# Self-attention inside a fused transformer block: heads that leave the matmul already turned

## The chip, the cores and the metric

The kernel runs on one core of a Trainium2 chip, as one launch. The metric is the device time in microseconds (us), the median of several executions.

## The reference

A block of 1024 tokens (32 sequences of 32 tokens, width 1024) in float32 passes through cross-attention, self-attention and a gated feed-forward part, each with a layer norm ahead of it and a residual sum behind it. The change is in the self-attention:

```python
q = (x @ Wq.T).reshape(B, S, H, dk).transpose(0, 2, 1, 3)     # 16 heads of 64
k = (x @ Wk.T).reshape(B, S, H, dk).transpose(0, 2, 1, 3)
v = (x @ Wv.T).reshape(B, S, H, dk).transpose(0, 2, 1, 3)
scores = jnp.einsum('bhqd,bhkd->bhqk', q, k) / jnp.sqrt(jnp.float32(dk))
scores = jnp.where(causal, scores, jnp.finfo(scores.dtype).min)
probs = jax.nn.softmax(scores, axis=-1)
attn = jnp.einsum('bhqk,bhkd->bhqd', probs, v)
attn = attn.transpose(0, 2, 1, 3).reshape(B, S, D)
return attn @ Wo.T
```

## The kernel before

**Tiling.** The tokens are 8 tiles (NT) of 128: four sequences of 32 tokens each. The 16 heads are 4 groups (NG) of four heads (HG). The loop over groups is a loop of the program for the first three; the last group is written out, because the layer norm of the feed-forward part (statistics, normalising, turning) is woven into it (`last`). Large matmuls take each operand as two parts of type fp32r, a high and a low one, and multiply them in three matmuls (`three`). The small ones of the attention (scores, attend, transposes) are in float32, and the trace records two passes for each float32 matmul, one for each transpose.

**A group on TensorE.** Queries and keys for all tokens (`job`, 24 matmuls of 512 columns each), then a pipeline over the tiles. In step st:

- `turn_heads(st - 2)`: two transposes of `o_sb`, into the second half of bank 4
- `scores(st)`: four heads, two passes each, stationary `qT`, moving `kT`, 64 rows of the array by turns
- `values(st + 1)`: v of the next tile, in bank 5
- `attend(st - 1)`: four heads, stationary the turned probabilities `att_z` (128 columns), moving `v` (64 columns), into the first half of bank 4
- `project(st - 2)`: 12 matmuls of 512 columns, `oT_hi` and `oT_lo` against the output weights, into banks 6 and 7

Step 7 has no `values`, and there `project(5)` stands ahead of `attend(6)`. After it come the first job of the next group, cut in two by `turn_heads(6)`, then `attend(7)`, `project(6)`, `turn_heads(7)`, the second job and `project(7)`. In the last group each step from 3 on ends with `norm_tile(st - 3)`, which turns a normalised tile.

**VectorE in step st** (all engines work through their queue in order, and wait on semaphores): `oT_lo` of tile st - 2, adding the causal mask to the scores (line 1446, four instructions), the row maximum (line 1451), a wait for ACT's exponentials, the turning of the probabilities (line 1461, four instructions), the reciprocal of the sums (line 1463), the division of the heads of tile st - 1 into `o_sb` (line 1473), and the addition of the projection of tile st - 2 to x (line 1481, two instructions), which frees banks 6 and 7 (`wo_free`). In the last group the statistics, part of the normalising and `xT_lo` come on top.

**ACT in step st:** `oT_hi` of tile st - 2 (line 687), the exponentials with their sums (line 669, four heads), the copy of v out of bank 5 (line 676), in some steps the high part of a weight tile.

A single `oT_hi` and `oT_lo` serve all tiles. The split of weights into low parts is GpSimd's.

Of the kernel before, what the change touches and what calls it, by code (L numbers as in the profile page):

```python
# [48 lines left out]
def build(nc, x_in, ctx_in, w_in, block_in, mask_in, ext_in, ext_t_in, out):  # L49
    stack = ExitStack()  # L50
    with stack:
# [74 lines left out]
        o_sb = sb(s, "o_sb", [P, HG * DK])  # L126
        oT_hi = sb(s, "oT_hi", [P, FT, P], F32R)
        oT_lo = sb(s, "oT_lo", [P, FT, P], F32R)
# [87 lines left out]
        o_ready = sem("o_ready")  # L216
        oT_psum = sem("oT_psum")
# [65 lines left out]
        TURNED_HEADS = slice(HG * DK, HG * DK + FT * P)  # L283
# [274 lines left out]
        def _(act):  # L558
# [104 lines left out]
            def group(g, last=False):  # L663
                def exps(st):

                    act.wait_ge(att_top_ready, g * 8 + (st + 1))
                    rowsof = flat3(att[st % 2])
                    for h in range(HG):
                        ins = act.activation(att_p[st % 2][:, h, :], rowsof[:, h * S:(h + 1) * S], ACT.Exp,  # L669
                                             bias=att_neg[st % 2][:, h:h + 1],  # L670
                                             accum_out=att_sum[st % 2][:, h:h + 1])
                    ins.then_inc(att_exp, 1)

                def keep_values(t):
                    act.wait_ge(v_done, g * 8 + (t + 1))
                    act.activation(v[:, t, :], ps[:, 5, 0:HG * DK], ACT.Copy).then_inc(v_kept, 1)

                keep_queries(g, 2)
                keep_queries(g, 3)
                pair_split(g, 2)  # L680
                act.wait_ge(k_done, g * 4 + 4)
                pair_split(g, 3)
                keep_values(0)
                for st in range(NT + 2):
                    if st >= 2:
                        act.wait_ge(oT_psum, g * 8 + (st - 1))
                        act.activation(flat(oT_hi[:, :, :]), ps[:, 4, TURNED_HEADS], ACT.Copy)\
                            .then_inc(oT_hi_done, 1)
                    if last and st >= 4:
                        turned_hi(2, st - 4)  # L690
                    if st < NT:
                        exps(st)
                    if st + 1 < NT:
                        keep_values(st + 1)
                    if last and st % 2 == 0 and st >= 4:
                        normalise(2, st - 3)
                    if st + 1 == NT - 1:
                        pair_split(g, 4)
                if not last:
                    keep_queries(g + 1, 0)  # L700
                    act.wait_ge(wo_done, (g + 1) * NT)
                    pair_split(g, 5)
                    keep_queries(g + 1, 1)
# [138 lines left out]
        def _(pe):  # L842
# [169 lines left out]
            def group(g, last=False):  # L1012
# [21 lines left out]
                def turn_heads(t):  # L1034

                    pe.wait_ge(o_ready, g * 8 + (t + 1))
                    for f in range(FT):
                        mm = pe.transpose(ps[:, 4, (FT + f) * P:(FT + f + 1) * P],
                                          o_sb[:, f * P:(f + 1) * P], ident[:, :])
                    mm.then_inc(oT_psum, 1)  # L1040

                def attend(t):
# [6 lines left out]
                    for h in range(HG):  # L1049
                        mm = pe.matmul(ps[:, 4, h * DK:(h + 1) * DK],  # L1050
                                       att_z[t % 2][:, (h % 2) * 2 + h // 2, :],
                                       v[:, t, h * DK:(h + 1) * DK], start=True, stop=True)
                    mm.then_inc(pv_done, 1)

                def project(t):
# [5 lines left out]
                    for f in range(FT):  # L1061
                        for half in range(2):
                            at = f * D + half * HALF
                            mm = three(ps[:, 6 + half, :], (oT_hi[:, f, :], oT_lo[:, f, :]),
# [15 lines left out]
                for st in range(2, NT):  # L1080
                    if st > 2:
                        turn_heads(st - 2)
                    pe.wait_ge(att_read, g * 8 + st)
                    scores(g, st)
                    if st == 2:
                        turn_heads(0)
                    if st < NT - 1:
                        values(st + 1)
                        attend(st - 1)
                        project(st - 2)  # L1090
                    else:
                        project(st - 2)
                        attend(st - 1)
# [7 lines left out]
                turn_heads(NT - 2)  # L1101
                mm = job(0, 0, 0, range(4, KD))
                if not last:
                    mm.then_inc(q_done, 1)
                attend(NT - 1)
                project(NT - 2)
                if last:
                    norm_tile(2, NT - 3)
                turn_heads(NT - 1)
                if last:  # L1110
                    job(1, 0, 1, range(0, 3))
                else:
                    job(1, 0, 1).then_inc(q_done, 1)
                project(NT - 1)
                if last:
                    norm_tile(2, NT - 2)

# [126 lines left out]
        def _(dve):  # L1244
# [182 lines left out]
            dve.memset(att_inv[0][:, :], 0.0).then_inc(wo_free, 1)  # L1427
            def group(g, last=False):
# [4 lines left out]
                for st in range(NT + 2):  # L1433
                    two = st % 2
                    if st >= 2:
                        dve.wait_ge(oT_hi_done, g * 8 + (st - 1))
                        dve.tensor_tensor(flat(oT_lo[:, :, :]), ps[:, 4, TURNED_HEADS],
                                          flat(oT_hi[:, :, :]).bitcast(F32), ALU.subtract)\
                            .then_inc(oT_ready, 1)
# [14 lines left out]
                    if last and st >= 4:  # L1454
                        turned_lo(2, st - 4)
                    if st < NT:
                        dve.wait_ge(att_exp, g * 8 + (st + 1))
                        for b in range(BT):
# [4 lines left out]
                        mark(dve.reciprocal(att_inv[two][:, :], att_sum[two][:, :]))  # L1463
                        settle()
# [4 lines left out]
                    if 1 <= st <= NT:  # L1469
                        dve.wait_ge(pv_done, g * 8 + st)  # L1470

                        by = att_inv[(st - 1) % 2][:, :].rearrange("p (e h) -> p h e", e=2)
                        dve.tensor_tensor(o_sb[:, :].rearrange("p (h e d) -> p h e d", h=2, e=2),
                                          ps[:, 4, 0:HG * DK].rearrange("p (h e d) -> p h e d", h=2, e=2),
                                          by.unsqueeze(3).broadcast_to([P, 2, 2, DK]), ALU.mult)\
                            .then_inc(o_ready, 1)
                    if st >= 2:
                        dve.wait_ge(wo_done, g * 8 + (st - 1))
                        for half in range(2):
                            part = x[:, st - 2, half * HALF:(half + 1) * HALF]  # L1480
                            ins = dve.tensor_tensor(part, ps[:, 6 + half, :], part, ALU.add)
                        ins.then_inc(wo_free, 1)
                        if last and st == NT + 1:
# [4 lines left out]
                        if last:  # L1488
                            dve.wait_ge(wo_free, g * 8 + st)
                            tile_stats(st - 2)  # L1490
# [153 lines left out]
GROUP_MARKS = 8  # L1644
# [82 lines left out]
```

## Time and profile before

| what | value |
|---|---|
| time, median of 3 runs | 1565.85 us (1565.71 to 1567.55) |
| profiled execution, time | 1564.08 us |
| its span, first to last instruction | 1562.3 us |
| TensorE busy | 97% of the span |
| VectorE, ACT, GpSimd busy | 51%, 34%, 54% |
| mean granted clock of TensorE | 0.997 |

The span is what the trace covers; the time is what the device reports for that same execution. Busy shares are means over the whole program. In the trace the matmuls of one line are pipelined, so each record lasts longer than the distance from its start to the next one's: costs on TensorE are read from start to start.

### The profile page before, as it was taken

To read this page: it belongs to the slowest core of one execution; us is meant where nothing else is said; L and a number is where in the kernel's file an instruction comes from. 1 tells how busy PE (TensorE), PEld (TensorE's weight loads), DVE (VectorE), ACT (ScalarE), POOL (GpSimd) and SP (SyncE) were. 2 spreads that over 40 slices of the span, in tenths; PEclk is the share of its full clock that TensorE was granted. 3 is DMA by queue.
4 is the path that set the end of the run, shared out by engine and by line. 5 is a ranking of instruction groups with operands and counts; after the bars stand their busy time and mean duration, and the time that the engine had idled before them with its cause. 6 is when DMAs were issued, how large, how long until landed. Compare 5 with 4: busy or idle time off the path is not lost.

```text
span 1562.3 us, 23574 instructions
## 1 busy us (share of the span) xinstructions
PE 1519.8 (97%) x8204; PEld 1246.1 (80%) x8204; DVE 795.9 (51%) x1249; ACT 536.7 (34%) x1093; POOL 851.4 (54%) x658
## 2 busy tenths in 40 slices
PE   6999899999999999989999999999999999999998
PEld 5667688888888887878888888888888888888886
DVE  4666516236145168694365365266266256256346
ACT  3334412222122133334334333433343443343342
POOL 0000220221211212167987987887887897897895
PEclk9999999999999999999999999999999999999999
DMA  9663210110100100011211211211211211111122
GB/s 367 261 243 149 108 54 29 54 54 19 61 27 27 54 1 1 21 34 54 74 47 42 72 47 54 60 47 54 60 51 49 60 54 47 60 54 49 58 60 107
DMA packets 41798, 110.42 MB, mean 71 GB/s; under 512 B 4672, under 2 KB 4800, under 8 KB 39328
## 3 DMA queue, kind: packets, MB, share of 16 engines
q1 hardware_dynamic: 41328, 109.07, 20.7%
q10 hardware_dynamic: 432, 0.82, 0.2%
q8 instruction: 27, 0.44, 0.1%
q14 instruction: 11, 0.09, 0.0%
HBM read 105.68 MB, written 4.19 MB: 70 GB/s over the span
## 4 chain that ended last, share of the span: by engine, by line
PE 89%; DVE 7%; ACT 1%; issue 1%; DMA 1%; SPq 0%; POOL 0%; DVEq 0%
PE ps L1212 36%; PE ps L1232 18%; PE ps L844 8%; PE ps L846 7%; PE ps L845 7%; PE ps L875 3%; PE ps L922 2%; PE ps L898 2%; PE ps L1050 1%; PE ps L850 1%; DVE t_raw L1533 1%; DMA x<-in_x 1%; ACT att_p L669 1%; DVE att L1446 1%; DVE att_z L1461 1%
## 5 line engine op out<-in xcount | busy, mean ns | idle before, releaser
L485 POOL TENSOR_TENSOR b_lo<-blk,b_hi 128x512 fp32r<-128x512 f32 x180 | 238.9, 1334 | 53.3 <-ACT b_hi L739 44.7
L454 POOL TENSOR_TENSOR w_lo<-raw,w_hi 128x2048 fp32r<-128x2048 f32 x18 | 83.5, 4640 | 325.7 <-ACT w_hi L604 325.7
L1616 DVE TENSOR_TENSOR x<-ps,x 128x1024 f32<-128x1024 f32 x210 | 242.2, 1210 | 0.0
L1212 PE MATMUL ps<-xT_hi,b_hi 128*128 128x512 f32 x480 | 187.0, 389 | 2.1 <-DVE x L1519 2.1
L1212 PE MATMUL ps<-xT_lo,b_hi 128*128 128x512 f32 x480 | 186.8, 389 | 0.0
L1212 PE MATMUL ps<-xT_hi,b_lo 128*128 128x512 f32 x480 | 186.7, 389 | 0.0
L1232 PE MATMUL ps<-b_hi,b_hi 128*128 128x512 f32 x420 | 166.7, 397 | 0.1
L1232 PE MATMUL ps<-b_lo,b_hi 128*128 128x512 f32 x420 | 163.7, 390 | 0.0
L1232 PE MATMUL ps<-b_hi,b_lo 128*128 128x512 f32 x420 | 163.6, 389 | 0.0
L1590 DVE TENSOR_TENSOR hid<-ps,kept 128x512 f32<-128x512 f32 x60 | 41.5, 691 | 229.6 <-PE ps L1212 189.7
L485 POOL TENSOR_TENSOR b_lo<-s_sum,b_hi 128x512 fp32r<-128x512 f32 x105 | 137.8, 1313 | 32.0 <-ACT b_hi L739 32.0
L1593 DVE TENSOR_TENSOR ps<-ps,kept 128x512 f32<-128x512 f32 x60 | 41.7, 694 | 181.7 <-PE ps L1212 152.8
L844 PE MATMUL ps<-xT_hi,w_hi 128*128 128x512 f32 x320 | 126.1, 394 | 0.0
L846 PE MATMUL ps<-xT_hi,w_lo 128*128 128x512 f32 x320 | 124.6, 390 | 0.0
L845 PE MATMUL ps<-xT_lo,w_hi 128*128 128x512 f32 x320 | 124.6, 389 | 0.0
L739 ACT ACTIVATE b_hi<-s_sum 128x512 fp32r<-128x512 f32 x105 | 66.1, 630 | 170.0 <-POOL s_sum L494 161.3
L739 ACT ACTIVATE b_hi<-blk 128x512 fp32r<-128x512 f32 x180 | 110.5, 622 | 22.6 <-PE ps L1212 19.7
L1212 PEld LDWEIGHTS ps<-xT_hi,b_hi 128*128 128x128 f32 x480 | 90.1, 188 | 21.6 <-DVE x L1519 2.9
L1212 PEld LDWEIGHTS ps<-xT_hi,b_lo 128*128 128x128 f32 x480 | 90.1, 188 | 18.7
L1212 PEld LDWEIGHTS ps<-xT_lo,b_hi 128*128 128x128 f32 x480 | 90.1, 188 | 18.7
L1232 PEld LDWEIGHTS ps<-b_hi,b_hi 128*128 128x128 f32 x420 | 78.8, 188 | 26.0 <-DVE x L1616 5.5
L762 ACT ACTIVATE kept<-ps 128x512 f32<-128x512 f32 x90 | 53.6, 596 | 131.9 <-PE ps L1212 131.9
(167 smaller groups left out, 3302.8 us busy)
## 6 DMA issues: line engine op xcount, KB each, us to landing
blk<-in_blocks SPq DMA_DIRECT2D x180, 256.0 KB, 2.7
ctx<-in_ctx SPq DMA_DIRECT2D x64, 512.0 KB, 9.4
raw<-in_w SPq DMA_DIRECT2D x19, 1024.0 KB, 4.8
x<-in_x SPq DMA_DIRECT2D x8, 512.0 KB, 4.1
out<-x SPq DMA_DIRECT2D x16, 256.0 KB, 2.6
xn<-in_ext ACTq DMA_DIRECT2D x3, 128.0 KB, 8.0
mask<-in_mask ACTq DMA_DIRECT2D x1, 288.0 KB, 6.7
extT<-in_ext_t ACTq DMA_DIRECT2D x1, 128.0 KB, 4.6
```

Of the source, the lines that this page charges most:

```text
L454: pool.tensor_tensor(w_lo[wslot][:, :], raw[slot][:, :], w_hi[wslot][:, :].bitcast(F32), ALU.subtract).then_inc(split_done[slot], 1)
L485: pool.tensor_tensor(b_lo[slot][:, :], src[:, :], b_hi[slot][:, :].bitcast(F32), ALU.subtract).then_inc(block_lo, 1)
L739: act.activation(b_hi[w_slot(n)][:, :], src[:, :], ACT.Copy).then_inc(block_hi, 1)
L762: act.activation(kept[i][:, :], ps[:, Y, :], ACT.Copy).then_inc(part_kept, 1)
L844: pe.matmul(dst, stat[0], moving[0], start=start, stop=False)
L845: pe.matmul(dst, stat[0], moving[1], start=False, stop=False)
L846: return pe.matmul(dst, stat[1], moving[0], start=False, stop=stop)
L875: mm = pe.transpose(ps[:, b, e * MB + m * P:e * MB + (m + 1) * P], ctx[t % RING][:, b, j // 2, m, at:at + P], ident[:, :])
L1212: mm = pe.matmul(ps[:, bank, :], stat[a], moving[b], start=first and m == 0, stop=(s == 3 and m == 2), skip_group_check=True)
L1232: mm = pe.matmul(ps[:, DOWN_BANKS[place] + i, :], stat[a], moving[b], start=DOWN_STARTS[place] and m == 0, stop=m == 2, skip_group_check=True)
L1593: dve.tensor_tensor(ps[:, Y + to, :], ps[:, Y + bank, :], kept[k][:, :], ALU.add)\
L1616: dve.tensor_tensor(part, ps[:, bank:bank + 2, :], part, ALU.add).then_inc(down_added, 1)
```

## The change

In `attend` the operands swap places: `v` of a head (64 columns) is stationary and the turned probabilities (128 columns) move, so that the result comes out as features by tokens, two heads above each other in the 128 partitions. `turn_heads`, `o_sb` and their semaphores go. VectorE divides the probabilities by their sum before it turns them, where it divided the heads afterwards. `oT_hi` and `oT_lo` get two buffers each. ACT copies `oT_hi` right behind `attend`, one step earlier in its order, and VectorE's `oT_lo` follows in the same step. In the first three groups the addition to x moves from the end of step st (tile st - 2) to the middle of the next (tile st - 3, behind the maximum); in the last group it stays. On TensorE `attend` stands ahead of `project` in all steps, the first job of the next group is cut differently, and `project(7)` comes ahead of the second job in the first three groups.

```diff
-        TURNED_HEADS = slice(HG * DK, HG * DK + FT * P)
+        HEADS = slice(0, FT * P)
...
                 for st in range(NT + 2):
-                    if st >= 2:
-                        act.wait_ge(oT_psum, g * 8 + (st - 1))
-                        act.activation(flat(oT_hi[:, :, :]), ps[:, 4, TURNED_HEADS], ACT.Copy)\
-                            .then_inc(oT_hi_done, 1)
...
                     if st + 1 < NT:
                         keep_values(st + 1)
+                    if 1 <= st <= NT:
+                        act.wait_ge(pv_done, g * 8 + st)
+                        act.activation(flat(oT_hi[(st - 1) % 2][:, :, :]), ps[:, 4, HEADS], ACT.Copy)\
+                            .then_inc(oT_hi_done, 1)
...
-                def turn_heads(t):
-
-                    pe.wait_ge(o_ready, g * 8 + (t + 1))
-                    for f in range(FT):
-                        mm = pe.transpose(ps[:, 4, (FT + f) * P:(FT + f + 1) * P],
-                                          o_sb[:, f * P:(f + 1) * P], ident[:, :])
-                    mm.then_inc(oT_psum, 1)
-
                 def attend(t):
...
                     for h in range(HG):
-                        mm = pe.matmul(ps[:, 4, h * DK:(h + 1) * DK],
-                                       att_z[t % 2][:, (h % 2) * 2 + h // 2, :],
-                                       v[:, t, h * DK:(h + 1) * DK], start=True, stop=True)
+                        r = slice((h % 2) * DK, (h % 2 + 1) * DK)
+                        mm = pe.matmul(ps[r, 4, (h // 2) * P:(h // 2 + 1) * P], v[:, t, h * DK:(h + 1) * DK],
+                                       att_z[t % 2][:, (h % 2) * 2 + h // 2, :], start=True, stop=True)
                     mm.then_inc(pv_done, 1)
...
                 for st in range(2, NT):
-                    if st > 2:
-                        turn_heads(st - 2)
                     pe.wait_ge(att_read, g * 8 + st)
                     scores(g, st)
-                    if st == 2:
-                        turn_heads(0)
                     if st < NT - 1:
                         values(st + 1)
-                        attend(st - 1)
-                        project(st - 2)
-                    else:
-                        project(st - 2)
-                        attend(st - 1)
+                    attend(st - 1)
+                    project(st - 2)
...
                 job(0, 0, 0, range(0, 4))
-                turn_heads(NT - 2)
-                mm = job(0, 0, 0, range(4, KD))
-                if not last:
-                    mm.then_inc(q_done, 1)
                 attend(NT - 1)
                 project(NT - 2)
+                mm = job(0, 0, 0, range(4, KD))
                 if last:
                     norm_tile(2, NT - 3)
-                turn_heads(NT - 1)
-                if last:
                     job(1, 0, 1, range(0, 3))
                 else:
-                    job(1, 0, 1).then_inc(q_done, 1)
+                    mm.then_inc(q_done, 1)
                 project(NT - 1)
                 if last:
                     norm_tile(2, NT - 2)
+                else:
+                    job(1, 0, 1).then_inc(q_done, 1)
...
+            def add_projected(g, t):
+                dve.wait_ge(wo_done, g * 8 + (t + 1))
+                for half in range(2):
+                    part = x[:, t, half * HALF:(half + 1) * HALF]
+                    ins = dve.tensor_tensor(part, ps[:, 6 + half, :], part, ALU.add)
+                ins.then_inc(wo_free, 1)
...
+                    if not last and st >= 3:
+                        add_projected(g, st - 3)
                     if st < NT:
                         dve.wait_ge(att_exp, g * 8 + (st + 1))
+                        mark(dve.reciprocal(att_inv[two][:, :], att_sum[two][:, :]))
+                        settle()
+                        mark(dve.tensor_tensor(att_p[two][:, :, :], att_p[two][:, :, :],
+                                               att_inv[two][:, :].unsqueeze(2).broadcast_to([P, HG, S]),
+                                               ALU.mult))
+                        settle()
                         for b in range(BT):
                             q = slice(b * S, (b + 1) * S)

                             ins = dve.transpose(att_z[two][q, :, b * S:(b + 1) * S], att_p[two][q, :, :])
                         ins.then_inc(att_turned, 1)
...
                     if 1 <= st <= NT:
...
+                        dve.wait_ge(oT_hi_done, g * 8 + st)
+                        dve.tensor_tensor(flat(oT_lo[(st - 1) % 2][:, :, :]), ps[:, 4, HEADS],
+                                          flat(oT_hi[(st - 1) % 2][:, :, :]).bitcast(F32), ALU.subtract)\
+                            .then_inc(oT_ready, 1)
+                    if last and st >= 2:
+                        add_projected(g, st - 2)
```

## Rows read from the trace of the kernel before

**Rows 1.** The page, busy time and share of the span

```profile
PE 1519.8 (97%) x8204; PEld 1246.1 (80%) x8204; DVE 795.9 (51%) x1249; ACT 536.7 (34%) x1093; POOL 851.4 (54%) x658
```

**Rows 2.** Busy time by stretch: start:end length, engines, granted clock, DMA

```profile
226.70:300.40 73.70, 71.70 (x481) 63.12 (x480) 37.89 (x111) 20.29 (x83) 9.17 (x2) 1.00 0.08 30
...
545.80:626.50 80.70, 75.21 (x523) 66.06 (x521) 60.07 (x150) 29.29 (x92) 15.63 (x23) 1.00 0.00 1
```

**Rows 3.** Timeline of TensorE, one step: start, length, instruction

```profile
250.54 1.00 PE L1050 MATMUL ps<-v,att_z 128*128 128x64 f32 x8
251.35 0.47 PE L844 MATMUL ps<-w_hi,oT_hi 128*128 128x512 f32 x1
...
254.21 0.38 PE L1038 MATMUL ps<-ident,o_sb 128*128 128x128 f32 x2
254.52 0.71 PE L1000 MATMUL ps<-kT,qT 64*128 64x128 f32 x8
255.16 0.39 PE L844 MATMUL ps<-w_hi,xT_hi 128*128 128x256 f32 x1
...
258.14 0.33 PE L1050 MATMUL ps<-v,att_z 128*128 128x64 f32 x2
```

**Rows 4.** Timeline of TensorE, step 2 of the first group

```profile
237.94 0.71 PE L1000 MATMUL ps<-kT,qT 64*128 64x128 f32 x8
239.81 0.44 PE L1038 MATMUL ps<-ident,o_sb 128*128 128x128 f32 x2 [1.15 <-DVE o_sb L1473]
240.00 0.36 PE L844 MATMUL ps<-w_hi,xT_hi 128*128 128x256 f32 x1
```

**Rows 5.** Groups by line, attention stage: total, mean ns, idle before

```profile
L1481 DVE TENSOR_TENSOR x<-ps,x 128x512 f32<-128x512 f32 x64 | 41.2, 684 | 50.8 <-PE ps L846 50.8
...
L1050 PEld LDWEIGHTS ps<-v,att_z 128*128 128x128 f32 x256 | 32.0, 192 | 0.6
L1000 PE MATMUL ps<-kT,qT 64*128 64x128 f32 x256 | 22.9, 297 | 0.0
...
L1473 DVE TENSOR_TENSOR o_sb<-ps,att_inv 128x256 f32<-128x256 f32 x32 | 13.6, 424 | 10.2 <-PE ps L1050 9.3
L1437 DVE TENSOR_TENSOR oT_lo<-ps,oT_hi 128x256 fp32r<-128x256 f32 x32 | 13.3, 416 | 9.5 <-ACT oT_hi L687 9.5
...
L687 ACT ACTIVATE oT_hi<-ps 128x256 fp32r<-128x256 f32 x32 | 12.3, 384 | 104.7 <-PE ps L1038 104.7
...
L1463 DVE RECIPROCAL att_inv<-att_sum 128x4 f32<-128x4 f32 x32 | 5.7, 178 | 1.0
```

**Rows 6.** Cross-attention's scores: loads by line, then TensorE's timeline

```profile
L898 PEld LDWEIGHTS ps<-cT,xt 128*32 128x32 f32 x512 | 14.9, 109 | 11.9 <-issue 3.6 <-ACT cT L572 1.0
...
118.60 1.93 PE L898 MATMUL ps<-cT,xt 128*32 128x256 f32 x32
120.46 0.33 PE L875 MATMUL ps<-ident,ctx 128*128 128x128 f32 x1
```

**Rows 7.** Timeline of step 7 of the first group, TensorE and VectorE

```profile
277.32 0.71 PE L1000 MATMUL ps<-kT,qT 64*128 64x128 f32 x8
...
278.74 1.18 DVE L1446 TENSOR_TENSOR att<-ps,causal 32x128 f32<-32x128 f32 x4
279.95 0.29 DVE L1451 TENSOR_REDUCE att_neg<-att 128x4 f32<-128x128 f32 x1
...
281.64 1.26 DVE L1461 STREAM_TRANSPOSE att_z<-att_p 32x128 f32<-32x128 f32 x4 [1.40 <-ACT att_p L669]
```

**Rows 8.** Waits, attention stage: total us, times, longest

```profile
PE ps L844 <- DVE oT_lo L1437: 4.6, 5, 1.7
```

**Rows 9.** Timeline of the last group, VectorE and TensorE

```profile
583.08 1.29 DVE L1481 TENSOR_TENSOR x<-ps,x 128x512 f32<-128x512 f32 x2 [0.30 <-PE ps L846]
...
600.35 1.29 DVE L1481 TENSOR_TENSOR x<-ps,x 128x512 f32<-128x512 f32 x2 [0.42 <-PE ps L846]
...
608.89 1.09 PE L850 MATMUL ps<-ident,xn 128*128 128x128 f32 x8 [1.24 <-DVE xn L1419]
```

More of the change, by code:

```diff
@@ L125, in build @@
         att_inv = [sb(s, f"att_inv{i}", [P, HG]) for i in range(2)]
-        o_sb = sb(s, "o_sb", [P, HG * DK])
-        oT_hi = sb(s, "oT_hi", [P, FT, P], F32R)
-        oT_lo = sb(s, "oT_lo", [P, FT, P], F32R)
+        oT_hi = [sb(s, f"oT_hi{i}", [P, FT, P], F32R) for i in range(2)]
+        oT_lo = [sb(s, f"oT_lo{i}", [P, FT, P], F32R) for i in range(2)]
         s.close()
@@ L215, in build @@
         pv_done = sem("pv_done")
-        o_ready = sem("o_ready")
-        oT_psum = sem("oT_psum")
         oT_hi_done = sem("oT_hi_done")
@@ L1063, in project @@
                             at = f * D + half * HALF
-                            mm = three(ps[:, 6 + half, :], (oT_hi[:, f, :], oT_lo[:, f, :]),
+                            mm = three(ps[:, 6 + half, :], (oT_hi[t % 2][:, f, :], oT_lo[t % 2][:, f, :]),
                                        (w_hi[1][:, at:at + HALF], w_lo[1][:, at:at + HALF]),
@@ L1432, in group @@
                         .then_inc(k_kept, 1)
-                for st in range(NT + 2):
+                for st in range(NT + (2 if last else 3)):
                     two = st % 2
[L1435 to L1439, printed above, removed]
                     if st < NT:
@@ L1462, in group @@
                         ins.then_inc(att_turned, 1)
-                        mark(dve.reciprocal(att_inv[two][:, :], att_sum[two][:, :]))
-                        settle()
                     if last and st % 2 and st >= 3:
@@ L1469, in group @@
                     if 1 <= st <= NT:
[L1470 to L1483, printed above, removed]
+                        dve.wait_ge(oT_hi_done, g * 8 + st)
[4 more added lines that the diff above has]
+                        add_projected(g, st - 2)
+                        if st == NT + 1:
                             dve.wait_ge(hi_done, ATT_PAIRS + 2)
@@ L1487, in group @@
                                               ALU.subtract).then_inc(split_done[1], 1)
-                        if last:
-                            dve.wait_ge(wo_free, g * 8 + st)
-                            tile_stats(st - 2)
+                        dve.wait_ge(wo_free, g * 8 + st)
+                        tile_stats(st - 2)
             dve.wait_ge(z_zero, 2)
@@ L1640, in _ @@
                         add(c, place, q)
-GROUP_MARKS = 8
+GROUP_MARKS = 16
 def flat(ap):
```

## Prediction

> **What bounds the kernel now.** I read the page first, then the busy times by stretch, then TensorE's instructions in order of time through one group of heads, and last the waits of the same stretch. The page puts TensorE at 97% busy over the whole span [rows 1], so a gain has to come out of its queue, or out of the 42 us in which it idles. By stretch, the attention part of each of the first three groups (from the first `values` to the last `project`) takes 73.7 us with 2.0 us idle, and that of the last group 80.7 us with 5.5 us idle; the granted clock is 1.00 [rows 2]. So the stage stands at full clock, the higher of its two levels, and is paced by TensorE.
>
> One inner step in order of time [rows 3] shows what that queue is made of, from start to start: attend 0.81 (250.54 to 251.35), project 2.86, turn_heads 0.31, scores 0.64, values 2.98 (255.16 to 258.14). Together 7.60 us, with no gap. Steps 3 to 6 of every group look like it, with a norm_tile more in the last group.
>
> **Removed: turn_heads.** 32 of them (8 tiles, 4 groups) at 0.31 us each: 9.9 us, 2.48 us a group. They stand bare on TensorE's path. With it goes the first one's wait: turn_heads(0) starts at 239.81, but scores(2) before it starts at 237.94 and needs 0.64, so TensorE was free at 238.58: 1.23 us a group [rows 4]. What takes its place is values(3), which needs bank 5 read by ACT, behind exps(1), behind VectorE. By the changed order VectorE finishes that chain about 0.3 us later than now (0.56 us added ahead of the first transposes, 0.21 taken from behind them), while TensorE arrives 0.17 us earlier: I take a new wait of 0.3 us. Net 0.9 us a group.
>
> **Changed: attend.** Now 4 heads, two passes each, so 8 records, with a 128-column stationary side and 64 moving columns. They run at 0.10 us a record, while a load of 128 columns lasts 0.192 and one of 32 columns 0.109 [rows 5, 6]: the loads seem to set the pace, not the columns that move. After: a stationary side of 64 columns, 128 moving, the heads alternating between the two column halves of the array. No row shows this form. The nearest is scores: also 8 records with 128 moving columns, alternating between two halves (of rows): 0.64 us [rows 3]. The readout's scores with 32-column stationary sides and 256 moving run 32 records in 1.86 us (118.60 to 120.46), 0.058 each [rows 6], twice the columns in half the time that attend's records take: column groups do overlap. I take 0.64, a saving of 0.17 an attend. Bounds: 8 x 0.058 = 0.46 below. Above, if the column halves do not overlap: the 8 records of scores are spread over 0.71 less 0.30 for the last one [rows 3, 5], 0.059 apart in two halves, so one half gives 0.118 a record; 8 x 0.118, plus the 0.17 us that scores takes beyond 8 x 0.059, is 1.11.
>
> The Trainium skill, TensorEngine Tiling (Array Packing), section Performance Considerations, recommends just this swap with column tiling where the moving side has 64 columns or fewer, for up to twice the speed; by that alone attend would take 0.41 us. The same page, section Key Properties, says that a change of tiling mode drains the engine, which speaks against it. Scores' 0.64, where its records alone make 0.47, agrees with the drain, so I side with the second sentence.
>
> **Moved on VectorE.** Per step the division of the heads goes, 0.424 us for 256 elements [rows 5]. The multiply of the probabilities comes. From 0.684 for 512 elements and 0.424 for 256 the slope is 1.0 ns an element, so 128 elements cost 0.29; with the two settles 0.35. The reciprocal (0.18, with its settle 0.21) moves ahead of the transposes. Total work: 0.07 us a step less. But the turned probabilities are 0.56 us later. In the first three groups that is covered: scores(st) ends at 0.7 us of the step, mask and maximum take to 2.3, exps 1.40 to 3.7 [rows 7], reciprocal and multiply to 4.3, transposes to 5.6; attend(st) wants them a whole step later, at about 11. oT_lo follows at 6.0, and the step is now 7.60 - 0.31 - 0.17 = 7.12 long. The cover is gone only if the multiply costs over a microsecond. ACT's copy of the heads (0.384) now waits for attend directly, behind keep_values, which is done before attend; nobody is queued behind it who is needed sooner.
>
> **Moved: add_projected(st - 3).** It now stands after the maximum, in the shadow of ACT's exps (1.29 against 1.40): free in steps 3 to 6. In step 7 there is no values to hide it. project(5) needs `wo_free` from add_projected(4), which was done in step 6 and is now queued behind mask and maximum of step 7. From the rows of step 7 [rows 7]: scores starts at 277.32, its results are there at 278.04, mask 1.18 and maximum 0.29 with their gaps to 279.55, the two additions to 280.84. TensorE, with attend(6) now ahead of project(5), is free at 277.32 + 0.64 + 0.64 = 278.60 and starts at about 280.9: 2.3 us idle. Today project(5) idles there for oT_lo, 0.9 us: the five waits of that kind hold 4.6 us, the longest, in the last group, 1.7 [rows 8]; of the rest three are these. That is 1.4 us a group lost. After it, project(6) comes 2.86 + 0.64 us and half a job (12 matmuls of 512 columns like project's, about 2.8) later and finds add_projected(5) done; the half job now between project(6) and project(7) covers ACT's copy, oT_lo and add_projected(6). Weight loads: split for K of the next group waits for project(7), as before, and now has the whole second job, some 5.6 us, more in front of K.
>
> **First three groups:** 2.48 + 8 x 0.17 (1.36) + 0.9 - 1.4 = 3.4 us each, 10.2 us in all.
>
> **Last group.** From step 3 on VectorE is the partner that sets the pace: its additions start at 583.08 and, two steps later, at 600.35, 17.27 us, with 0.30 and 0.42 us idle before these two [rows 9], since statistics, normalising and xT_lo are added. There only VectorE's own saving counts: about 0.1 us a step, 0.5 us to norm_tile(4). Ahead of the first norm_tile I take 1.5 us (two turn_heads 0.62, three attends 0.51, the first wait 0.9, less 0.5 that goes back into the wait for normalising). After norm_tile(4): turn_heads(6) and (7) 0.62, attend(7) 0.17, the wait of project(7) about 0.4: 1.2. Sum 3.2. norm_tile(4), which waits 1.24 now [rows 9], should wait 3 to 4 us, since project(5)'s own wait before it vanishes while VectorE's queue does not shorten.
>
> **Sum.** 10.2 + 3.2 = 13.4 us faster. The profiled execution took 1564.08 us, 1.8 beyond its span of 1562.3 and 1.8 below the median of the runs, 1565.85; so 1550.7 for an execution like it, and 1552.4 for the median, which I predict.
>
> **Rivals.**
> *Attend at the lower bound (0.46).* For it: the overlap in the readout. Against: scores, the nearer form, has the changeover. About 21 of the 32 attends count (attend(0) and attend(6) are swallowed by the waits behind them, most of the last group by VectorE): 21 x 0.18 = 3.8 more, 1548.6. By the page's factor of two it would be 21 x 0.23 = 4.8 more, 1547.6.
> *No overlap of the halves (1.11).* 21 x 0.47 = 9.9 less: 3.5 faster, 1562.3. Against it speaks [rows 6].
> *VectorE eats more.* If multiply and settles cost 0.6 instead of 0.35, or ACT's new order delays the normalising, each late start costs TensorE in the first steps and all through the last group: 0.25 us at about 10 places and in three times step 7: 3 to 5 us less, 1556.
> *Slower: the loads are no longer hidden.* If in column mode a load cannot run beside the other half's matmul, each of the 8 records costs its 0.118 and the load of 64 columns (0.109 us for 32 columns and 0.192 for 128 give 0.00086 a column, so 0.055), 0.173 in all; with the changeover attend takes 1.55 us. The gain is used up at 0.64 + 13.4/21 = 1.28 us. At 1.55 it is 21 x 0.27 = 5.7 us slower, 1571.5. Against: the readout's 0.058 a record includes its loads.
>
> **Chances.** Forecast 0.70; lower bound or the page's two 0.10; no overlap 0.09; VectorE more 0.06; slower 0.04; and 0.01 that several of these cancel. What a measurement of this kernel can tell is 0.2%, 3.1 us. All but the last two are faster: 0.94; within it 0.02; slower 0.04. Range: 1547 takes in the lower bound; 1560.5 takes in VectorE's rival and reaches toward no overlap. Outside it lie no overlap, slower and some of the forecast's own tails, not quite 2 in 10.
>
> **What would show it.** After: no transposes of heads; inner steps of 7.1 us; eight attend records within 0.64 us to the next start; project(5) idle 2.3 us in three groups, released by the addition to x; first idle of about 0.3 us before values(3); norm_tile(4) waiting 3 to 4 us. The prediction is wrong if attend takes over 0.8 us, if TensorE idles in steps 3 to 6 of the first groups, or if VectorE's multiply is much over 0.3 us.

## The result and the profile after

The changed kernel takes 1558.13 us (median of 5 runs, 1557.48 to 1561.55) against 1565.71 us before (5 runs): ratio 0.9955, 95% interval 0.994 to 0.9969. A second set of runs beside the experiments gave 1560.75 (8 runs) against 1564.70, ratio 0.9972 (0.9961 to 0.9982). So it is 4 to 8 us faster, where 13.4 was forecast; the span of the profiled execution fell from 1562.3 to 1555.8 us. Where the two sets differ is told under a0_changed.

The page of the kernel after answers to [rows 1]:

```profile
PE 1512.2 (97%) x8140; PEld 1227.3 (79%) x8140; DVE 795.2 (51%) x1249; ACT 537.4 (35%) x1093; POOL 851.4 (55%) x658
```

64 matmul records fewer are the transposes of the heads; VectorE's work is the same. The mean granted clock is 0.992, where it was 0.997.

One inner step of TensorE after (start, length, instruction), to be read beside [rows 3]:

```profile
248.78 0.66 PE L1040 MATMUL ps<-att_z,v 128*64 128x128 f32 x8
249.37 0.50 PE L841 MATMUL ps<-w_hi,oT_hi 128*128 128x512 f32 x1
...
252.33 0.71 PE L997 MATMUL ps<-kT,qT 64*128 64x128 f32 x8
252.97 0.39 PE L841 MATMUL ps<-w_hi,xT_hi 128*128 128x256 f32 x1
...
256.02 0.44 PE L1040 MATMUL ps<-att_z,v 128*64 128x128 f32 x4
```

From start to start: attend 0.59 (was 0.81), project 2.96 (2.86), no turn_heads (0.31), scores 0.64, values 3.05 (2.98). The step is 7.24 us (7.60). What attend gained is partly given back by its neighbours: project before scores, and values before attend, take 0.1 and 0.07 us longer.

Step 7 of the first group after, TensorE and VectorE in order of time, beside [rows 7]:

```profile
274.07 0.71 PE L997 MATMUL ps<-kT,qT 64*128 64x128 f32 x8
274.71 0.66 PE L1040 MATMUL ps<-att_z,v 128*64 128x128 f32 x8
274.83 1.19 DVE L1428 TENSOR_TENSOR att<-ps,causal 32x128 f32<-32x128 f32 x4 [2.10 <-PE ps L997]
276.06 0.29 DVE L1433 TENSOR_REDUCE att_neg<-att 128x4 f32<-128x128 f32 x1
276.37 1.29 DVE L1412 TENSOR_TENSOR x<-ps,x 128x512 f32<-128x512 f32 x2
277.74 0.18 DVE L1442 RECIPROCAL att_inv<-att_sum 128x4 f32<-128x4 f32 x1
277.81 0.47 PE L841 MATMUL ps<-w_hi,oT_hi 128*128 128x512 f32 x1 [2.44 <-DVE x L1412]
...
278.80 0.41 PE L842 MATMUL ps<-w_lo,oT_hi 128*128 128x512 f32 x1
279.03 0.61 PE L843 MATMUL ps<-w_hi,oT_lo 128*128 128x512 f32 x1
279.44 0.63 PE L841 MATMUL ps<-w_hi,oT_hi 128*128 128x512 f32 x1
279.86 0.63 PE L842 MATMUL ps<-w_lo,oT_hi 128*128 128x512 f32 x1
...
282.42 0.41 PE L842 MATMUL ps<-xT_lo,w_hi 128*128 128x512 f32 x1
```

project(5) waits for the addition to x, as forecast, 2.44 us. What was not forecast stands behind it: from 279.03 on the matmuls start 0.43 us apart instead of 0.23, until 282.42. The busy times by stretch say why (the third number from the end is the granted clock):

```profile
278.00:279.00 1.00, 1.00 (x5) 0.83 (x5) 0.94 (x4) 0.00 (x0) 0.01 (x1) 1.00 0.00 0
279.00:282.40 3.40, 3.40 (x9) 2.61 (x8) 1.10 (x4) 0.00 (x0) 0.00 (x0) 0.51 0.86 308
```

The clock stood at 1.2 GHz, the lower of its two levels, for 3.4 us, which cost 1.6 us. The engine had idled 2.44 us just before. The same is seen in the third group and, after the wait before norm_tile(4), in the last; not in the second, whose wait is as long (2.43 us). In the last group, by TensorE's timeline:

```profile
602.11 1.09 PE L847 MATMUL ps<-ident,xn 128*128 128x128 f32 x8 [3.52 <-DVE xn L1398]
...
603.67 0.63 PE L843 MATMUL ps<-xT_hi,w_lo 128*128 128x512 f32 x1
604.10 0.63 PE L841 MATMUL ps<-xT_hi,w_hi 128*128 128x512 f32 x1
```

The sum, by groups. From the first `values` of one group to that of the next: 106.36 us before, three times; after, 105.29, 103.69 and 105.31. The middle one, without a fall of the clock, is 2.67 shorter. The last group is 1.6 us shorter (89.97 to 88.36, to its norm_tile(7)), 3.2 without the fall. Together 3 x 2.67 + 3.2 = 11.2 us of gain, less 3 falls of the clock of about 1.6: 6.4. The span fell by 6.5.

### The profile page after: what moved, and what is told of

It is laid out like the page before. It is cut to its first block, busy times and chain, and to the rows that moved or that the text cites. A ratio compares the mean times of both kernels' runs of the same rounds, so it can differ in the third digit from the quotient of the medians.

```text
span 1555.8 us, 23467 instructions
## 1 busy us (share of the span) xinstructions
PE 1512.2 (97%) x8140; PEld 1227.3 (79%) x8140; DVE 795.2 (51%) x1249; ACT 537.4 (35%) x1093; POOL 851.4 (55%) x658
## 4 chain that ended last, share of the span: by engine, by line
PE 90%; DVE 7%; ACT 1%; DMA 1%; issue 1%; SPq 0%; POOL 0%; DVEq 0%
PE ps L1191 37%; PE ps L1211 18%; PE ps L841 8%; PE ps L842 8%; PE ps L843 8%; PE ps L872 3%; PE ps L919 2%; PE ps L895 2%; PE ps L847 1%; DVE t_raw L1513 1%; PE ps L997 1%; DMA x<-in_x 1%; PE ps L1040 1%; PE ps L882 1%; DVE att L1428 1%
```

## Experiments

All times beside the kernel before on the same chip; the ratio is time after by time before, with its 95% interval. Edits are to the changed kernel if nothing else is said. No edit touches what comes ahead of the first `values` of the self-attention, and yet that starts at 225.88 us in one profiled execution and at 229.54 in another. So two profiles are compared by the time from the first `values` to the end of the span: 1335.6 us in the kernel before (1562.3 less 226.71), 1329.0 in the changed one (1555.8 less 226.82). A table behind the last experiment has all of them.

**e1_fill: something to do in the gaps.**

```diff
+                def fill(n):
+                    pe.wait_ge(v_kept, g * 8 + NT)
+                    for i in range(n):
+                        pe.matmul(ps[:, 5, :], w_hi[1][:, 0:P], w_hi[1][:, 0:HALF], start=True, stop=True)
...
                     attend(st - 1)
+                    if st == NT - 1 and not last:
+                        fill(8)
                     project(st - 2)
+                    if st == NT - 1 and last:
+                        fill(13)
```

Expected: 

> The changed kernel with matmuls that nobody reads in its two longest waits of TensorE: 8 of 512 columns between attend(6) and project(5) in the first three groups, 13 between project(5) and norm_tile(4) in the last. Theory 'idle': the granted clock falls because TensorE stands idle there (2.4 and 3.5 us), and the 12 matmuls behind the wait then run at up to 0.43 us apart; with the gaps filled the clock stays at 1.00 in all four places and the kernel is 3 to 5 us faster than the changed one (1558.1), about 1554, mean clock 0.997. Rival 'column form': the small attends lower the clock, not the gap; then it still falls there, mean clock 0.992, time 1558 as before. In both the fills themselves cost under 0.5 us.

Measured: 1553.35 us, ratio 0.9927 (0.9914 to 0.9939); clock 0.997. The waits of the attention stage, as totals, times and longest, and the first of these places by stretch:

```profile
PE ps L841 <- DVE x L1421: 1.2, 3, 0.4
```

```profile
270.00:300.00 30.00, 29.61 (x148) 23.32 (x143) 10.81 (x27) 7.35 (x16) 9.18 (x2) 1.00 0.12 39
```

More work on the critical engine made the kernel about 5 us faster; from the first `values` on it is 4.8 us less than in the changed kernel, which is three falls of the clock at 1.6 us. project(5) starts no sooner after scores(7) than without the fill (3.74 us in both), so what was won is the clock alone: 1.00 behind all four places, with attend in its new form all the while. Theory "idle" holds; that the form of the matmuls alone lowers the clock does not.

**e2_add_early: take the wait away.**

```diff
+                    if not last and st == NT - 1:
+                        add_projected(g, st - 3)
                     if st < NT:

                         dve.wait_ge(att_done, g * 8 + (st + 1))
...
-                    if not last and st >= 3:
+                    if not last and st >= 3 and st != NT - 1:
                         add_projected(g, st - 3)
```

Expected: 

> The changed kernel, but in step 7 of the first three groups the addition of tile 4 stands ahead of the mask instead of behind the maximum. Theory: project(5) waits for this addition alone. Then its wait falls from 2.4 to about 0.3 us, 2.1 a group, and with the gap goes the fall of the clock behind it (about 1.5 us in two of three groups): 8 to 10 us faster than the changed kernel, about 1549. Rival: oT_lo or another wait takes its place at project(5) or at attend(7) and project(6), since mask and maximum of step 7 come 0.8 us later: then under 3 us faster, 1555 or more.

Measured: 1548.78 us, ratio 0.9898 (0.9883 to 0.9912), 9 us below the changed kernel's first result. By the timeline of TensorE:

```profile
277.14 0.66 PE L1040 MATMUL ps<-att_z,v 128*64 128x128 f32 x8
278.04 0.47 PE L841 MATMUL ps<-w_hi,oT_hi 128*128 128x512 f32 x1 [0.24 <-DVE x L1412]
```

The wait is 0.24 us in each of the three groups, the clock 1.00 through all of them, and nothing took its place. The mean clock of this execution is 0.994 all the same: the first 60 us, which the edit does not touch, ran at 0.94. From the first `values` on, the profile is 11.5 us shorter than that of the changed kernel: 6.6 for the waits and 4.8 for three falls of the clock. One of these three stood behind norm_tile(4), whose wait (3.51 us) is as long as it was; that the clock kept its level there is not the edit's doing as far as the runs show.

**e3_old_operands: the form of attend by itself.**

```diff
-                        mm = pe.matmul(ps[r, 4, (h // 2) * P:(h // 2 + 1) * P], v[:, t, h * DK:(h + 1) * DK],
-                                       att_z[t % 2][:, (h % 2) * 2 + h // 2, :], start=True, stop=True)
+                        mm = pe.matmul(ps[:, 4, h * DK:(h + 1) * DK],
+                                       att_z[t % 2][:, (h % 2) * 2 + h // 2, :],
+                                       v[:, t, h * DK:(h + 1) * DK], start=True, stop=True)
```

Expected: 

> The changed kernel with attend's operands as they were (probabilities stationary, v moving) and all else as changed. Left out: the heads do not come out turned, so what is projected is not the reference's. It measures the column form by itself. Theory: the form saves about 0.13 us an attend, changeovers included (0.81 before, 0.59 plus 0.09 in front after), at about 21 places: this one is some 3 us slower than the changed kernel, 1561, and the wait at project(5) is 0.2 us shorter; the clock falls behind it as in the changed kernel, mean 0.992. Rival 'column form lowers the clock': the clock stays at 1.00 and the time is 1556 or less.

Measured: 1563.24 us, ratio 0.9990 (0.9981 to 0.9999). The step is 7.35 us instead of 7.25 (project(0) of the first group starts at 245.21, project(4) at 274.62, four steps on), so the new form is worth 0.10 us an attend: 2.1 us over the 21 that count. The clock fell in all three groups behind a wait of 1.99 us, and in the last, with the old form of attend in place: one fall, 1.6 us, more than in the first profile of the changed kernel. So the form is not needed for the fall either.

**e4_no_multiply: VectorE's new work.**

```diff
-                        mark(dve.tensor_tensor(att_p[two][:, :, :], att_p[two][:, :, :],
-                                               att_inv[two][:, :].unsqueeze(2).broadcast_to([P, HG, S]),
-                                               ALU.mult))
-                        settle()
```

Expected: 

> The changed kernel without the multiply of the probabilities by their reciprocal sums and its settle (0.35 us a step on VectorE); the reciprocal stays. Left out: the division of the softmax. Theory: in the first three groups the multiply is covered, so TensorE's steps stay at 7.25 us and project(5)'s wait at 2.4; in the last group VectorE sets the pace and it gives about 0.35 us in each of four or five steps: 1.5 us faster than the changed kernel, about 1556.5. Rival: the later turned probabilities are what keeps the gain below the forecast: 4 us or more faster, 1554 or less.

Measured: 1556.78 us, ratio 0.9946 (0.9934 to 0.9959): 1.3 to 4 us below the two results of the changed kernel. Steps of 7.25 us in the first groups as before, and the wait of project(5) by the table of waits

```profile
PE ps L841 <- DVE x L1412: 7.3, 3, 2.4
PE ps L847 <- DVE xn L1398: 4.2, 2, 3.2
```

is the same to a tenth (7.3 us in three times in the changed kernel too). The multiply is covered there; in the last group the waits for normalising are 0.3 to 0.5 us shorter each. In this profile the clock fell in all four groups, one fall more than in that of the changed kernel, and from the first `values` on both take the same to 0.2 us: without that fall it would be about 1.4 us less, as expected. A latency 0.35 us shorter in every step does not bring the missing gain.

**e7_move_alone: the moved addition in the kernel before.** Edit to the kernel before, nothing else of the change:

```diff
-                for st in range(NT + 2):
+                for st in range(NT + (2 if last else 3)):
...
+                    if not last and st >= 3:
+                        add_projected(g, st - 3)
                     if st < NT:
                         dve.wait_ge(att_exp, g * 8 + (st + 1))
...
-                    if st >= 2:
-                        dve.wait_ge(wo_done, g * 8 + (st - 1))
+                    if last and st >= 2:
+                        add_projected(g, st - 2)
```

Expected: 

> The kernel before with one part of the change alone: in the first three groups the addition to x stands one step later, behind the maximum. Theory: project(5) in step 7 now waits for it, from 277.96 to about 281.6 us of the trace of before, 3.6 us where it was 0.9, and the clock falls behind such a wait in most groups (1.5 us each time): 8 to 13 us slower than before, about 1574 to 1578, mean clock 0.992 or less. Rival: the move is hidden by the exponentials in all steps: within 1 us of before.

Measured: 1575.92 us, ratio 1.0079 (1.0065 to 1.0093): 11 us slower. By TensorE's timeline:

```profile
280.42 0.47 PE L844 MATMUL ps<-w_hi,oT_hi 128*128 128x512 f32 x1 [3.11 <-DVE x L1433]
...
281.52 0.63 PE L845 MATMUL ps<-w_lo,oT_hi 128*128 128x512 f32 x1
281.95 0.63 PE L846 MATMUL ps<-w_hi,oT_lo 128*128 128x512 f32 x1
```

3.1 us of wait where there were 0.9, and the slow matmuls behind it in all three groups. In this kernel no record of attend has the new form, and the clock falls. It fell in the last group as well, behind the wait of 1.73 us that the kernel before has too.

**a0_changed: the changed kernel once more.**

Expected: 

> The changed kernel as it is, on the same chip as the three others, to compare them with. Both theories: 0.9955 of before, mean clock 0.992 or so, the wait before project(5) 2.4 us in three groups, with the clock lower behind most of them; which of the places show the lower clock may differ from the first profile.

Measured: 1560.75 us, as told above; clock 0.990. Busy times by stretch of the second and third groups' project(5), and of the first 60 us:

```profile
387.00:391.50 4.50, 4.50 (x21) 3.38 (x21) 1.29 (x2) 0.00 (x0) 0.00 (x0) 0.87 0.34 144
492.00:497.00 5.00, 5.00 (x24) 3.75 (x23) 1.29 (x2) 0.00 (x0) 0.00 (x0) 0.80 0.33 141
...
0.00:60.00 60.00, 46.79 (x416) 35.54 (x416) 31.79 (x59) 20.69 (x43) 4.21 (x18) 0.94 0.86 329
```

Here the first group kept its clock and the second lost it, the other way round from the first profile. The waits are the same to 0.01 us. So whether a given wait costs the clock differs between executions of one program. It is not what sets these two profiles apart, though: each has two falls at project(5) and one at norm_tile(4). Of the 3.4 us between their spans, 2.5 stand ahead of the self-attention, whose first `values` starts at 229.33 instead of 226.82; the clock of the first 60 us is 0.94 here and 1.00 there. From that point on they take 1329.9 and 1329.0 us, 5.7 and 6.6 less than the kernel before. Whether the same lies behind the medians of the two sets was not tested.

**e5_norm_early: VectorE's order in the last group.** On top of e2_add_early:

```diff
+                    if last and st % 2 and 3 <= st < NT:
+                        if st > 3:
+                            dve.wait_ge(xt_psum, NT + st - 4)
+                        normalise(2, st - 3)
                     if st < NT:
                         dve.wait_ge(att_exp, g * 8 + (st + 1))
...
-                    if last and st % 2 and st >= 3:
+                    if last and st % 2 and st >= NT:
```

Expected: 

> The kernel of e2_add_early, and in the last group VectorE normalises (steps 3, 5 and 7) right behind xT_lo, ahead of its wait for the exponentials, instead of behind the turning of the probabilities. Theory: in the last group VectorE's order decides when norm_tile(4) can start; the normalising comes about 1.9 us sooner, the wait of 3.5 us before norm_tile(4) falls to about 1.6, those before norm_tile(0) and (2) go down as well: 2 to 4 us faster than e2_add_early, ratio to before about 0.987. Rival: the probabilities turned 0.8 us later make attend wait in the steps behind: no gain, ratio 0.990.

Measured: 1545.00 us, ratio 0.9882 (0.9867 to 0.9898). The interval overlaps e2's; from the first `values` on the profile is 1.8 us shorter, where 2 to 4 were expected, and the trace says what moved. The wait before norm_tile(0) is gone, but the one before norm_tile(4) is 3.17 us where 1.6 was expected. TensorE's, VectorE's and GpSimd's timelines of that place:

```profile
589.53 0.66 PE L847 MATMUL ps<-ident,xn 128*128 128x128 f32 x4 [3.17 <-DVE xn L1398]
...
588.66 0.81 DVE L1398 TENSOR_SCALAR xn<-x,mean_var,rstd 128x1024 f32<-128x1024 f32 x1 [1.40 <-POOL shift L446]
...
582.90 4.59 POOL L451 TENSOR_TENSOR w_lo<-raw,w_hi 128x2048 fp32r<-128x2048 f32 x1 [5.15 <-ACT w_hi L601]
587.46 0.55 POOL L440 TENSOR_TENSOR rstd<-mean_var,minus_half 128x1 f32<-128x1 f32 x1
```

The expectation missed an engine: the scale of tile 4 is queued on GpSimd behind a split of 4.59 us. VectorE's early turn only makes it wait there.

**e6_attend_next: scores and attend side by side.** On top of e5:

```diff
+                    attend(st - 1)
                     if st < NT - 1:
                         values(st + 1)
-                    attend(st - 1)
                     project(st - 2)
```

Expected: 

> The kernel of e5_norm_early with attend(st - 1) directly behind scores(st), ahead of values(st + 1), so that the two kinds of matmul that use part of the array stand next to each other. Theory 'changeover': each change between whole-array and part-array matmuls costs about 0.1 us beyond the records (values to attend 0.09, project to scores 0.09); the step has four now and two or three after, so it shrinks from 7.25 to 7.10 us or less: 1.5 to 3 us faster in all, ratio to before about 0.9855. Rival: scores and attend use the array in different halves (rows, columns) and the change between them costs the same: no difference, step 7.25 us.

Measured: 1554.96 us, ratio 0.9939 (0.9925 to 0.9952): 10 us slower than e5, and yet the step is shorter. TensorE's timeline of the first group:

```profile
241.07 0.66 PE L1040 MATMUL ps<-att_z,v 128*64 128x128 f32 x8 [2.06 <-DVE oT_lo L1465]
...
242.52 0.41 PE L841 MATMUL ps<-w_hi,xT_hi 128*128 128x256 f32 x1
243.16 0.41 PE L841 MATMUL ps<-w_hi,xT_hi 128*128 128x256 f32 x1
...
248.96 0.72 PE L997 MATMUL ps<-kT,qT 64*128 64x128 f32 x8
249.60 0.66 PE L1040 MATMUL ps<-att_z,v 128*64 128x128 f32 x8
...
256.01 0.71 PE L997 MATMUL ps<-kT,qT 64*128 64x128 f32 x8
```

The step is 7.05 us (248.96 to 256.01), 0.2 less than with values between: theory "changeover" holds. But attend(1) in step 2 now waits 2.06 us in each group for oT_lo of tile 0, and behind it, in the first group, the matmuls of values stand 0.64 instead of 0.36 apart for three: the clock again. It fell so in the last group too, and a third time behind norm_tile(4), where e5 with the same wait of 3.17 us kept it. Four waits of 2.06 us and three falls at 1.6 are 13 us; the shorter steps give some of it back.

**e8_norm4_later and e9_next_from3: two repairs.** e8, on top of e5, moves norm_tile(4) of the last group behind the half job; e9, on top of e8, puts attend next to scores from step 3 on only.

```diff
-                    if last and st >= 3:
+                    if last and 3 <= st < NT - 1:
                         norm_tile(2, st - 3)
...
                 job(0, 0, 0, range(0, 4))
+                if last:
+                    norm_tile(2, NT - 4)
                 attend(NT - 1)
```

Expected of e8: 

> The kernel of e5_norm_early with norm_tile(4) of the last group behind the first half job instead of ahead of it. Theory: in e5 two things end at nearly the same time, GpSimd's split of the gate weights (587.49 in its trace) and, behind it in GpSimd's queue, the scale of tile 4, so that norm_tile(4) starts only at 589.5 with the job behind it. The half job needs the split alone and can start at 587.6, norm_tile(4) then finds its tile ready: TensorE's wait falls from 3.2 to about 1.4 us, 1.8 to 2 us faster than e5, and 1.5 more in executions in which the clock fell there: ratio to before about 0.9865. Rival: VectorE's queue behind (xT_lo of tile 4, wanted later by one half job) becomes late in turn: no difference to e5, 0.988.

Expected of e9: 

> The kernel of e8_norm4_later with attend(st - 1) directly behind scores(st) in steps 3 to 7, and behind values(3) in step 2 as in the changed kernel. Theory: e6_attend_next had the shorter step (7.05 against 7.25 us) and lost it again to one wait, attend(1) in step 2, 2.06 us for oT_lo of tile 0, and to the clock behind it; without that wait 4 steps x 0.2 us x 3 groups, 2.4 us and some in the last group, are left: 2 to 3 us faster than e8, ratio to before about 0.985. Rival: the shorter step makes VectorE or ACT late elsewhere (a wait of TensorE in steps 3 to 6 of the first groups): no difference to e8.

Measured: e8 1542.49 us, ratio 0.9868 (0.9851 to 0.9885); e9 1542.86, ratio 0.9859 (0.9841 to 0.9877). TensorE's timeline of e8:

```profile
587.64 0.50 PE L841 MATMUL ps<-xT_hi,w_hi 128*128 128x512 f32 x1 [1.18 <-POOL w_lo L451]
590.51 1.03 PE L847 MATMUL ps<-ident,xn 128*128 128x128 f32 x8
591.86 0.66 PE L1040 MATMUL ps<-att_z,v 128*64 128x128 f32 x8 [0.31 <-DVE oT_lo L1467]
593.05 0.47 PE L841 MATMUL ps<-w_hi,oT_hi 128*128 128x512 f32 x1 [0.54 <-DVE x L1414]
```

The wait of 3.17 became 1.18, and 0.85 of the 2.0 came back in two short waits behind it: VectorE is late in turn, as the rival said, but only by a part. That is 1.1 us less, and so is the time from the first `values` on (1314.6 against 1315.7); the rest of the 2.5 us between the medians of e5 and e8 is not shown to be the edit's. In e9 the steps of the first groups are 7.05 us with no wait in them. Of the 0.8 us a group a part went into the next thing that is late: the half job behind project(5) now starts at 280.51, where GpSimd's split for it (275.79, 4.59 long) ends at 280.38. The two versions cannot be told apart by their times; from the first `values` on e9's profile is 1.2 us shorter, about half of what was expected. Each is about 21 us below the kernel before and 16 to 18 below the changed one.

**All profiled executions side by side.** First `values` is where the self-attention's first `values` starts; falls are places from there to norm_tile(7) of the last group where the granted clock stood at its lower level.

| run | first `values`, us | from there to the end, us | falls |
|---|---|---|---|
| before | 226.71 | 1335.6 | 0 |
| after | 226.82 | 1329.0 | 3 |
| a0_changed | 229.33 | 1329.9 | 3 |
| e1_fill | 225.88 | 1324.2 | 0 |
| e2_add_early | 229.24 | 1317.5 | 0 |
| e3_old_operands | 229.54 | 1333.6 | 4 |
| e4_no_multiply | 226.08 | 1329.2 | 4 |
| e5_norm_early | 226.05 | 1315.7 | 0 |
| e6_attend_next | 227.32 | 1326.4 | 3 |
| e7_move_alone | 225.97 | 1348.1 | 4 |
| e8_norm4_later | 226.12 | 1314.6 | 0 |
| e9_next_from3 | 229.41 | 1313.4 | 0 |

## Why the prediction was right or wrong

Direction and range held (1547 to 1560.5, forecast 1552.4, measured 1558.13); the second set of runs, 1560.75, lies just beyond the range. 13.4 us were forecast and 7.6 came, 4.0 in the second set. That the range held was partly luck: its slow end was set for VectorE's rival, and what took the time was something else. (The terms of a group add up to 3.34; written as 3.4, they count 0.2 too much in three groups.) Step by step:

- **turn_heads, 0.31 each:** gone, but only about 0.22 of each was its own. The rest, 0.09, was the changeover in front of scores, which project now pays (2.96 instead of 2.86; 2.94 in e3, where attend has its old form). This changeover was in the row and was read as the transposes' cost.
- **attend, 0.64:** 0.59 for its records, and 0.07 to 0.1 in front of it. Net 0.15 saved by these rows and 0.10 by e3, instead of 0.17. The column halves do overlap; "no overlap" and "loads no longer hidden" are out.
- Both terms together make the step 7.24 instead of 7.12: 0.13 a step, 0.65 a group, 2 us in all. This is the term that was mis-sized in the undisturbed part (2.67 a group instead of 3.4). The cost of a changeover was taken from scores' own row alone, while part of it stands in the neighbours' rows; e6 shows it the other way round, 0.2 a step when the two forms stand side by side.
- **The first wait:** 0.3 us before values(3) were forecast, there is none (scores(2) at 237.79, values(3) at 238.46). Slightly better than said.
- **VectorE's multiply:** 0.292 us measured, 0.29 forecast; covered in the first groups, as said (e4).
- **project(5) in step 7:** 2.3 forecast, 2.44 measured, released by the addition, in all three groups. The mechanism was right, and its wait alone was priced at 1.4 us a group. **The step that failed is that price:** it counted the idle time and not what idle time does to TensorE's clock. Each fall costs 1.6 us, in two of three groups, and once more behind norm_tile(4), whose wait (3 to 4 us forecast, 3.52 measured) was also seen and also priced as a wait only. That is 4.8 of the 7 us missing. e1 (filled: 4.8 us back from the first `values` on), e2 (wait removed: 11.5 back, of which 6.6 are 3 x 2.2 us of wait) and e7 (old form of attend, the same fall) show it from three sides.
- **Last group, 3.2:** 3.2 without the fall of the clock.

The chances gave 0.70 to the forecast's case and none to the clock, though the rows of before showed a clock of 1.00 in this stage [rows 2] with waits of up to 1.7 us in it [rows 8]: it could have been asked what waits of 2.3 and 3.5 us do to it. The trace of before holds a case, 31 us behind norm_tile(7), in the feed-forward part:

```profile
663.63 0.39 PE L846 MATMUL ps<-xT_hi,w_lo 128*128 128x512 f32 x1
666.78 0.47 PE L844 MATMUL ps<-w_hi,h_hi 128*128 128x512 f32 x1 [2.76 <-issue]
...
668.23 0.63 PE L846 MATMUL ps<-w_hi,h_lo 128*128 128x512 f32 x1
668.66 0.63 PE L844 MATMUL ps<-w_hi,h_hi 128*128 128x512 f32 x1
```

```profile
667.00:672.00 5.00, 5.00 (x16) 3.94 (x16) 4.30 (x4) 2.39 (x4) 0.80 (x1) 0.66 0.06 9
```

Behind 2.76 us of idle time the matmuls stand 0.43 us apart for a while, with matmuls of 512 columns on both sides of the wait and none of the attention's small ones near. The same idle time is followed by a fall in eleven of the twelve profiled executions, all but e7's. So what such a wait can cost could be read before the change was made.

On the Trainium skill, TensorEngine Tiling (Array Packing): its section Performance Considerations recommends the swap, and its section Theoretical Speedup gives it at most twice the speed. This case gives less: attend's 8 records went from 0.81 to 0.59, and to 0.68 with the 0.09 us by which the last matmul of values ahead of them is longer. Its section Key Properties says that a change of tiling mode drains TensorE. The runs agree for a change from whole-array matmuls to scores or attend, about 0.1 us each. They show no such cost from scores' form to attend's in e6, which is a change of mode too: scores takes 0.64 us (248.96 to 249.60), as ahead of values.

Left open: what decides whether one wait costs the clock and the next does not. Waits of 2.0 to 3.1 us before project(5) cost it in 13 of 15 places (after, a0, e3, e4, e7), those of 3.2 to 3.5 us before norm_tile(4) in 5 of 7 (not in e2 and e5), those of 2.06 us in e6 in 2 of 4. One of 1.73 us in the last group of e7 cost it, and the same wait in the kernel before did not. In two places, the last group of a0 and the third of e7, the clock stayed low for about twice the 3.4 us. What lowered the clock in the first 60 us of some executions is open too.

## What to carry to other kernels

When an edit opens a wait of some two or three microseconds on a TensorE that otherwise rarely rests, price it at the wait plus a fall of the clock behind it, here 1.6 us in 13 of 15 such places at project(5), and look in the trace of before for what a wait of that length does. Look for the instruction that could stand elsewhere in the one step where its cover is missing (e2: one addition moved ahead of the mask, 6.6 us of waits and the falls of the clock behind them). When two executions are compared, first see whether they differ ahead of the change: here up to 3.7 us did. A part-array form pays a changeover on either side, part of which is booked under its neighbours, so compare whole steps, and put such forms side by side. And a stall that is repaired on one engine should be followed into every queue that the value passes through: here GpSimd's, behind a split.

## What the runs showed of the hardware that was not expected

- The granted clock of TensorE fell to the lower level, mostly for 3.4 us, behind single waits of 1.7 to 3.5 us, and the 12 matmuls of 512 columns of project(5) then took 4.2 to 4.4 us instead of 2.84. Behind waits of 0.24 to 0.4 us in the same place (e1, e2) it stayed at 1.00.
- Matmuls whose result nobody reads, 8 of them (2.1 us) in each of three gaps and 13 in a fourth, made the kernel about 5 us faster (7 beside the second set of the changed kernel).
- A change from whole-array matmuls to scores' or attend's form costs about 0.1 us, seen in the last record ahead of it (values 0.21 instead of 0.12 us, project 0.32 instead of 0.23); scores and attend side by side save 0.2 us a step (e6, e9).
- Float32 matmuls with 64 stationary columns on alternating column halves: 8 records with 128 moving columns each in 0.59 us, their loads 0.136 us long, against 0.109 for 32 columns and 0.192 for 128.
